# Two-layer graph network with norms: the end of the last two groups, with one table of means and variances and one chain of scale for both

## The reference, cut to what matters

```python
x = _layernorm(x + _L0_gnn_ref(x, adj, L0_gnn_weight, L0_gnn_bias), axis=-1)
x = _layernorm(x + _L1_gnn_ref(x, adj, adj, ...), axis=-1)      # no learned scale

def _L0_gnn_ref(x, adj, weight, bias):
    return jnp.einsum('bnd,do->bno', jnp.einsum('nm,bmd->bnd', adj, x), weight) + bias

def _L1_gnn_ref(x, in_mat, out_mat, ...):                        # in_mat = out_mat = adj
    h = x
    for _ in range(3):
        a_in = jnp.einsum('nm,bmd->bnd', in_mat, h)
        a_out = jnp.einsum('nm,bmd->bnd', out_mat, h)
        av = jnp.concatenate([a_in, a_out], axis=-1)
        z = jax.nn.sigmoid(_lin(av, w3_w, w3_b) + _lin(h, u3_w, u3_b))
        r = jax.nn.sigmoid(_lin(av, w4_w, w4_b) + _lin(h, u3_w, u3_b))
        hv = jnp.tanh(_lin(av, w5_w, w5_b) + _lin(r * h, u5_w, u5_b))
        h = (1.0 - z) * h + z * hv
    return h

def _layernorm(x, axis=-1, eps=1e-05):
    return (x - x.mean(axis, keepdims=True)) / jnp.sqrt(x.var(axis, keepdims=True) + eps)
```

## Time and profile before

| | |
|---|---|
| time, median of 3 runs | 1602.59 us (1601.28 to 1603.81) |
| the profiled execution's own time | 1604.63 us |
| its span from first to last instruction | 1602.0 us |
| mean granted TensorE clock | 0.997 of full speed |
| TensorE matmul busy | 1584.9 us, 99% of the span |
| VectorE, ScalarE, GpSimd busy | 87%, 72%, 21% |
| HBM read and written | 149.89 MB and 146.28 MB |

### The profile page before, as it was taken

The page is one execution under the profiler, slowest core; times in us unless marked ns, Lnnn a source line. Parts: engine busy times, 40 slices in busy tenths (PEclk is TensorE's granted clock), DMA queues, the critical chain, the costliest instruction groups (busy, mean ns, idle before and its releaser), DMA issues.

```text
span 1602.0 us, 21857 instructions
## 1 busy us (share of the span) xinstructions
PE 1584.9 (99%) x7404; PEld 1327.0 (83%) x7404; DVE 1393.0 (87%) x1413; ACT 1151.9 (72%) x2302; POOL 339.1 (21%) x390
## 2 busy tenths in 40 slices
PE   9999999999999999999999999999999999999996
PEld 8888888888888888888888888888888888888885
DVE  6888888889889888988989889898888898888887
ACT  4677667768777777776787677776777777776666
POOL 5111111223121221212212122212132121210013
PEclk9999999999999999999999999999999999999998
DMA  5646545775557664676636676466755576456545
GB/s 183 184 160 195 172 146 182 221 220 195 153 186 222 211 195 133 198 223 211 197 134 196 210 221 187 155 197 214 221 162 169 188 220 211 135 154 197 169 147 157
DMA packets 215760, 297.63 MB, mean 186 GB/s; under 512 B 21217, under 2 KB 184033, under 8 KB 215649
## 3 DMA queue, kind: packets, MB, share of 16 engines
q1 hardware_dynamic: 215232, 295.92, 59.5%
q10 hardware_dynamic: 416, 0.33, 0.1%
HBM read 149.89 MB, written 146.28 MB: 185 GB/s over the span
## 4 chain that ended last, share of the span: by engine, by line
PE 83%; DMA 6%; DVE 5%; SPq 3%; issue 1%; ACT 1%; POOL 0%; POOLq 0%; DVEq 0%; ACTq 0%
PE ps_r L453 42%; PE ps_h L453 28%; PE ps_a L541 7%; PE ps_l L498 4%; SPq L311 3%; DMA h_scratch_a<-h_blocks_a 2%; PE ps_l L508 2%; DMA h_scratch_b<-h_blocks_b 1%; DVE hv L1074 1%; DVE a_blocks L1034 1%; DMA a_landed<-a_scratch_b 1%; DVE h_blocks_b L1089 1%; DVE hv L1071 0%; DMA bias_row<-b 0%; DMA h_scratch<-h_blocks 0%
## 5 line engine op out<-in xcount | busy, mean ns | idle before, releaser
L1034 DVE STREAM_TRANSPOSE a_blocks<-ps_a 128x1024 f32<-128x1024 f32 x92 | 114.8, 1248 | 89.5 <-PE ps_a L541 89.4
L815 ACT ACTIVATE rh<-ps_r,bias_r 128x512 f32<-128x512 f32 x192 | 127.9, 683 | 76.7 <-PE ps_r L453 74.3
L654 ACT ACTIVATE rh_hi<-rh 128x512 fp32r<-128x512 f32 x192 | 119.0, 632 | 77.0 <-DVE rh L1062 77.0
L827 ACT ACTIVATE z_sb<-ps_r,bias_z 128x512 f32<-128x512 f32 x192 | 126.1, 680 | 35.5 <-PE ps_r L453 34.5
L1074 DVE TENSOR_TENSOR hv<-hv,z_sb 128x1024 f32<-128x1024 f32 x95 | 126.7, 1334 | 10.6 <-DVE hv L1071 0.9
L916 DVE TENSOR_TENSOR rh_lo<-rh,rh_hi 128x512 fp32r<-128x512 f32 x192 | 125.7, 689 | 9.4
L831 ACT ACTIVATE hv<-ps_h,bias_h 128x512 f32<-128x512 f32 x192 | 121.1, 676 | 11.9 <-PE ps_h L453 11.9
L453 PE MATMUL ps_r<-a_hi_a,w_hi 128*128 128x512 f32 x384 | 118.9, 391 | 0.6 <-ACT rh L815 0.5
L453 PE MATMUL ps_h<-rh_hi,u_hi 128*128 128x512 f32 x384 | 118.8, 390 | 0.1
L453 PE MATMUL ps_r<-h_hi,u_hi 128*128 128x512 f32 x384 | 118.7, 390 | 0.2
L453 PE MATMUL ps_r<-a_lo_a,w_hi 128*128 128x512 f32 x384 | 118.4, 389 | 0.4 <-DVE a_lo_a L916 0.4
(11 more groups left out here) (389 smaller groups left out, 4298.5 us busy)
## 6 DMA issues: line engine op xcount, KB each, us to landing
h_scratch_a<-h_blocks_a SPq DMA_DIRECT2D x48, 512.0 KB, 5.0
h_landed_a<-h_scratch_a SPq DMA_DIRECT2D x192, 128.0 KB, 2.8
h_scratch_b<-h_blocks_b SPq DMA_DIRECT2D x47, 512.0 KB, 4.2
h_landed_b<-h_scratch_b SPq DMA_DIRECT2D x188, 128.0 KB, 3.1
a_scratch_a<-a_blocks SPq DMA_DIRECT2D x46, 512.0 KB, 2.7
a_landed<-a_scratch_a SPq DMA_DIRECT2D x184, 128.0 KB, 2.9
a_scratch_b<-a_blocks SPq DMA_DIRECT2D x46, 512.0 KB, 2.7
a_landed<-a_scratch_b SPq DMA_DIRECT2D x184, 128.0 KB, 3.0
```

The costliest lines, as they stand in the source:

```text
L654: return act.activation(dst, src, ACT.Copy)
L815: act.activation(rh[:, c, :], ps_r[:, c, :], ACT.Sigmoid, bias=bias_r[:, c:c + 1]).then_inc(r_ready, 1)
L827: act.activation(z_sb[:, c, :], ps_r[:, c, :], ACT.Sigmoid, bias=bias_z[:, c:c + 1]).then_inc(z_ready, 1)
L1034: tr = dve.transpose(flat_blocks(a_blocks).rearrange("p (x e) -> p x e", e=Q), flat(ps_a).rearrange("p (x f) -> p x f", f=Q))
```

## The change

Groups 30 and 31 get one table `end_meanvar` of 128 x 8 pairs (columns 0 to 3 for group 30, 4 to 7 for group 31). ScalarE writes the variances of group 30 into it, GpSimd their means (one new operation, -16 times `out_neg_mean`), and VectorE both numbers of group 31. One GpSimd chain of four operations on 128 x 8 numbers follows, in place of two chains on 128 x 4. VectorE and ScalarE work on group 31 first, and then on group 30: of group 30 VectorE norms three batches and ScalarE one. SyncE issues the store of group 31's half ahead of group 30's store.

```diff
+        end_meanvar = sb("end_meanvar", [P, 2 * G, 2])
+        end_var_eps, end_rstd, end_mean_rstd, end_shift = (sb(f"end_{n}", [P, 2 * G])
+                                                           for n in ("var_eps", "rstd", "mean_rstd", "shift"))
...
             store_last()
+            store(LAST - 1)
...
             def last_norm():
                 act.wait_ge(last_shift, 1)
...
+                    nm = act.activation(last_result[:, b, :], by_node(ps_l)[:, b, :], ACT.Identity,
+                                        bias=end_shift[:, G + b:G + b + 1], scale=end_rstd[:, G + b:G + b + 1])
                 nm.then_inc(last_out, 1)
+                g = LAST - 1
+                act.activation(result_batch(g, 0), rows_of(result_rows(g), 0), ACT.Identity, bias=end_shift[:, 0:1],
+                               scale=end_rstd[:, 0:1]).then_inc(out_ready, 1)
                 act.wait_ge(last_out, 1)
                 act.dma_start(out_groups[LAST][:, G // 2:G, :], last_result[:, G // 2:G, :]).then_inc(last_stored, 16)
...
-                g, rows = LAST - 1, result_rows(LAST - 1)
-                dve.wait_ge(late_shift, 1)
-                dve.wait_ge(out_stored[g % 2], (g // 2) * 16)
-                for b in range(G // 2, G):
-                    nm = dve.tensor_scalar(result[g % 2][:, b, :].rearrange("p (c i f) -> p c i f", c=C, f=Q),
...
+            def last_rows():
+
                 dve.wait_ge(last_var, 1)
                 dve.wait_ge(last_rstd, 1)
                 for b in range(G // 2):
...
                 nm.then_inc(last_half, 1)
+                g = LAST - 1
+                dve.wait_ge(late_mean, 1)
+                dve.wait_ge(out_spread_ready, LATE + 1)
+                for b in range(1, G):
+                    nm = dve.tensor_scalar(result_batch(g, b), rows_of(result_rows(g), b), end_meanvar[:, b, 0:1],
+                                           end_rstd[:, b:b + 1], ALU.subtract, ALU.mult)
+                nm.then_inc(late_half, 1)
...
                 if s == SLOTS:
                     centre(out_pass, LATE, out_summed, out_centred)
-                    scale_of_passes(late_norm, out_pass, LATE, out_spread_ready, out_eps_added, out_rstd_ready, out_scaled,
-                                    late_shift)
+                    pool.wait_ge(out_centred, LATE + 1)
+                    pool.tensor_tensor(end_meanvar[:, 0:G, 0], out_pass[1][:, :], minus_sixteen[:, :],
+                                       ALU.mult).then_inc(late_mean, 1)
...
-            scale_and_shift(h0_norm, 0, last_var, last_var_eps, last_rstd, last_mean, last_shift, None, 0)
+            pool.wait_ge(out_spread_ready, LATE + 1)
+            pool.wait_ge(last_var, 1)
+            pool.tensor_tensor(end_var_eps[:, :], end_meanvar[:, :, 1], eps[:, :], ALU.add).then_inc(last_var_eps, 1)
+            pool.wait_ge(last_var_eps, 1)
+            pool.tensor_tensor(end_rstd[:, :], end_var_eps[:, :], minus_half[:, :], ALU.pow).then_inc(last_rstd, 1)
+            pool.wait_ge(last_rstd, 1)
+            pool.wait_ge(late_mean, 1)
+            pool.tensor_tensor(end_mean_rstd[:, :], end_meanvar[:, :, 0], end_rstd[:, :],
+                               ALU.mult).then_inc(last_mean, 1)
+            pool.wait_ge(last_mean, 1)
+            pool.tensor_tensor(end_shift[:, :], end_mean_rstd[:, :], minus_one[:, :], ALU.mult).then_inc(last_shift, 1)
```

More of the change, by code:

```diff
@@ L126, in gnn_kernel @@
         ident = sb("ident", [P, P])
-        minus_half, minus_one, eps = sb("minus_half", [P, G]), sb("minus_one", [P, G]), sb("eps", [P, G])
+        minus_half, minus_one, eps = (sb(n, [P, 2 * G]) for n in ("minus_half", "minus_one", "eps"))
+        minus_sixteen = sb("minus_sixteen", [P, G])
         w0_raw = sb("w0_raw", [P, C, D])
@@ L429, in _ @@
                 for g in result_at(s, STORE, LAST_STORE):
-                    store(g)
+                    if g < LAST - 1:
+                        store(g)
                 if (g := group_at(s, TURN, -2)) is not None and g >= FOUR + 2:
@@ L746, in result_norm @@
             def result_norm(g):
[L748 to L751, removed]
+                act.wait_ge(out_shift, g + 1)
                 if g >= 2:
                     act.wait_ge(out_stored[g % 2], (g // 2) * 16)
-                _, _, _, rstd, _, shift = out_norm if g < LAST - 1 else late_norm
-                for b in range(G if g < LAST - 1 else G // 2):
+                _, _, _, rstd, _, shift = out_norm
+                for b in range(G):
                     nm = act.activation(result[g % 2][:, b, :].rearrange("p (c i f) -> p c i f", c=C, f=Q),
@@ L1130, in last_statistics @@
                 for b in range(G):
[L1131 removed]
+                    mv = dve.bn_aggr(end_meanvar[:, G + b, :], sums[:, b, :])
                 mv.then_inc(last_var, 1)
[L1133 to L1140 removed]
+            def last_rows():
                 dve.wait_ge(last_var, 1)
@@ L1216, in _ @@
                     last_statistics()
+                    last_rows()
         @block.gpsimd
@@ L1255, in scale_of_passes @@
                 pool.wait_ge(spread_ready, n + 1)
-                pool.tensor_tensor(var_eps[:, :], spread[:, :], eps[:, :], ALU.add).then_inc(eps_added, 1)
+                pool.tensor_tensor(var_eps[:, :], spread[:, :], eps[:, 0:G], ALU.add).then_inc(eps_added, 1)
                 pool.wait_ge(eps_added, n + 1)
-                pool.tensor_tensor(rstd[:, :], var_eps[:, :], minus_half[:, :], ALU.pow).then_inc(rstd_ready, 1)
+                pool.tensor_tensor(rstd[:, :], var_eps[:, :], minus_half[:, 0:G], ALU.pow).then_inc(rstd_ready, 1)
                 pool.wait_ge(rstd_ready, n + 1)
@@ L1268, in scale_and_shift @@
                     pool.wait_ge(used, earlier)
-                pool.tensor_tensor(var_eps[:, :], meanvar[:, :, 1], eps[:, :], ALU.add).then_inc(eps_added, 1)
+                pool.tensor_tensor(var_eps[:, :], meanvar[:, :, 1], eps[:, 0:G], ALU.add).then_inc(eps_added, 1)
                 pool.wait_ge(eps_added, g + 1)
-                pool.tensor_tensor(rstd[:, :], var_eps[:, :], minus_half[:, :], ALU.pow).then_inc(rstd_ready, 1)
+                pool.tensor_tensor(rstd[:, :], var_eps[:, :], minus_half[:, 0:G], ALU.pow).then_inc(rstd_ready, 1)
                 pool.wait_ge(rstd_ready, g + 1)
@@ L1274, in scale_and_shift @@
                 pool.wait_ge(mean_ready, g + 1)
-                pool.tensor_tensor(shift[:, :], mean_rstd[:, :], minus_one[:, :], ALU.mult).then_inc(shift_ready, 1)
+                pool.tensor_tensor(shift[:, :], mean_rstd[:, :], minus_one[:, 0:G], ALU.mult).then_inc(shift_ready, 1)
             def first_scale(g):
```

23 lines of the change are left out of this document (11 added, 12 removed).

## The result

The changed kernel takes 1613.65 us (median of 6 runs, 1613.36 to 1615.76) against 1603.2 (6 runs, 1601.28 to 1604.09): a ratio of 1.007, 95% interval 1.006 to 1.0079. It is slower by some 10 us, where I forecast no difference that can be measured and a range up to 1605.0.

The account below looks back on a forecast made before the run. The prediction took TensorE to bound the slots, untouched by the change, and the draining store bytes to bound the end. Gaps in the stores added 0.3 us to 1602.59, giving 1602.9 us, range 1600.8 to 1605.0.

Parts of the forecast that it names:

- what bounds the kernel: Whole span: TensorE has the slots, which the change leaves untouched; its effect lies in the last 10 us, a draining store queue.
- the new tables shift the places of other tiles: Rival, in the 96 slots: moved SBUF tiles change each slot's time; 33 ns per slot would be 3.2 us; chance 0.04.
- The terms of the end: Last 10 us: power, scale time, store issues and gaps in the stores, together 0.2 to 0.4 us, taken as 0.3.
- the gap: DMA queue at the end: stores pause 0.19 us before group 31's first half, or 0.22 before ScalarE's half.
- P: GpSimd's joint chain at the end: duration of the power on 128 x 8, taken as 1.8 us, between 1.01 and 2.02.
- R: GpSimd's joint chain at the end: time the scale is ready, 1594.32 + P, 1596.12 with P = 1.8.
- The issue times: Last stores: group 31's first half R + 1.14, ScalarE's R + 1.64 or R + 2.13, group 30's R + 2.21.
- the chain, a rival at 0.10: Rival, at the end: the last store issue sets the end, so the time would be 1601.7 to 1602.5 us; chance 0.10.
- my 0.3: End of the kernel: time added by gaps in the stores, 0.3 us, from a sum of 0.2 to 0.4.
- The rival that the power is dearer than twice its price: Rival, GpSimd's power at the end: at 4.04 us the kernel takes 1605.0 us; chance 0.06.

Follow-up runs that it names:

- experiment 10: Changed kernel with 224 unused bytes ahead of `w0_raw`, large tiles 256 bytes from their old place, against the kernel before: 1602.71 us against 1602.56, ratio 1.0004.

## Why the prediction was wrong

The step that failed is the first, in what bounds the kernel: that the change "does not touch an instruction" of the slots, and "Whatever it does happens in the last 10 us". The first half is true and the second doesn't follow. I had the mechanism as a rival, that the new tables shift the places of other tiles, and gave it 0.04 because "Nothing in the rows speaks for it". It needed 33 ns per slot to matter and has 99. I named a new constant of the change only for its 0.10 us at the start, and its 32 bytes did the harm. What the runs showed in its place: the shift takes the adjacency matmuls from 389 to 395 ns and some around them with them, and padding alone reproduces the whole loss (1613.66 against 1613.65 us). The rows of one profile can't show what a shift costs, because in it every tile stands where it stands. But the declaration in the diff showed that one would occur, and TensorE's 1487.16 of 1488.00 us showed that anything that slows a matmul comes out in full.

The terms of the end held but for one, the gap. P was 1.64 us where I took 1.8 between 1.01 and 2.02. Four columns more cost 0.63 us, 0.16 each. The Trainium skill, GPSIMD Engine Reference, section "Elementwise — side-by-side cycle accounting", has 2.6 cycles per element, which would be an estimated 9 ns for four; the trace doesn't agree for a power. R came 5.94 us after the transposes begin where I had 5.91, partly by luck: P was 0.16 shorter, and the joint chain began 0.19 later (4.02 us after the transposes begin, against 3.83). The issue times held within 0.1 us, and the stores end by what the DMA engines still have to move: the last issue came at 8.08 us after the transposes where it had been at 8.21, and the span closed at 11.9 where it was 11.8. So the chain, a rival at 0.10, didn't bind.

The mis-sized term of the end is the gap: 0.2 forecast, 0.75 in the changed kernel's profile. I took group 29's store at its time in one profile, while it depends on when GpSimd's `out_neg_mean` ends, 0.51 or 1.25 us after the transposes begin, and the later case is the rarer one. With the early start the end costs 0.8 us in one pair of profiles. In the time of the kernel (experiment 10) that can't be told from my 0.3.

The rival that the power is dearer than twice its price fell: 1.64 with VectorE idle. No tried version beats the kernel before beyond what a measurement can tell.

## What to carry to other kernels

When a change adds or widens a tile, compare the places of all tiles in the two programs before anything else, above all if TensorE is the bound. A constant can be padded so that weights and streamed tiles keep their distance within 256 bytes (the 224 bytes of experiment 10), or declared behind the large tiles instead of ahead of them, which wasn't tried here. A change of a few instructions at the end that costs the same in every slot isn't in these instructions: cut the span by windows at a landmark of the program, then look at the shortest and longest duration of one tile's matmuls. An experiment with only an unused tile separates place from work in one run.

## What the runs showed of the hardware

In this kernel a 128 x 512 fp32 matmul takes 389 ns when the loaded tiles and the streamed ones stand at the same place within 256 bytes, and mostly a few ns more otherwise. The adjacency matmuls have medians of 394 to 396 at 32 bytes, 388 to 394 at 64, 391 to 399 at 96, 392 to 398 at 128, and 389 again at 256. It comes in a fixed pattern over the matmuls of a sequence. At 32 bytes matmuls around the mismatched ones are slow too, one ahead and five of the seven behind, so that 6 of them in a slot (12 in 28 of the slots) made about 14 slow on average; at 64 bytes those behind are not. The Trainium skill, SBUF — State Buffer, section "Operand start alignment", asks only that an operand start at a multiple of its element size; all the tiles here do, and the section has no price. Which part of the reading of the tiles makes the cost wasn't tried: all runs move whole tiles of fp32 numbers, and none moves the reads within a tile.

The same small GpSimd operation (128 x 4) took 0.20 us in the changed kernel's profile and 0.68 in that of the kernel before, where it ran beside an operation of VectorE. A power on 128 x 8 took 1.64 us, on 128 x 4 1.01. And ScalarE's queue issued a store at 1607.35 while the operation ahead of it ran from 1607.21 to 1607.80; the store had no wait on that operation.
